# Two-layer transformer block on one core: the first layer's down product with tokens on partitions, gates applied in the scalar engine's copies

## The chip, the cores and the metric

The kernel runs on one core of a Trainium2 chip. The metric is device time in microseconds (us) of one execution. The median of three runs of the kernel before is 1977.41 us (1973.36 to 1984.65). The engines are named as the profile names them: PE is TensorE, DVE is VectorE, ACT is ScalarE, POOL is GpSimd, SP issues the DMAs.

## The reference

There are 16 sequences of 512 tokens with 128 features. Four residual steps follow one another, each on a layer norm of its input:

```
x = x + linear_attention(layernorm(x))         # layer 0: 16 heads of 8
x = x + experts0(layernorm(x))                 # layer 0: 8 routed experts, 2 of them per token, and 2 shared ones
x = x + softmax_attention(layernorm(x))        # layer 1: keys after the query are masked
x = x + experts1(layernorm(x))                 # layer 1: 16 experts, each takes its 512 best tokens
```

The change lies in the second step. With `xt` the normed tokens it is

```
scores  = softmax(xt @ gate_w.T)
_, idx  = top_k(scores + gate_bias, 2)
weights = take_along_axis(scores, idx)
for e in range(8):
    gate_e = sum(where(idx == e, weights, 0))                # one number per token
    h      = silu(xt @ w1[e].T) * (xt @ w3[e].T)
    y      = y + gate_e[:, None] * (h @ w2[e].T)
z = (silu(xt @ sw1.T) * (xt @ sw3.T)) @ sw2.T                # two shared experts of width 128, no gate
```

## The kernel before, in words

One sequence (512 tokens, four tiles of 128) is the unit of work. The kernel is written engine by engine with semaphores, and the order on each engine is the order of the code. Three stages of three sequences run side by side in two alternating phases. The helper `looped` writes the first and last phases out and puts the rest into a hardware loop of 13 turns, which holds one `x_phase` and one `y_phase`; at its end each engine jumps back, 12 times in all.

In `x_phase(f, b, t, g)` sequence `f` goes through the ten experts of layer 0, sequence `b` through the first pass of its attention scores (40 fills of three PSUM banks `ba`, each followed by row maxima on DVE, `maxima`), sequence `t` ends its attention (output product, rms norm, router logits) and sequence `g` starts (layer norm, transposes). In `y_phase(b, f, r, t)` sequence `b` makes its scores a second time with the maxima subtracted, ACT takes the exponentials and PE the outputs; `f` does its linear attention and, on DVE, the gates of its experts (`f_logits`, `f_gates`, `f_rank`); `r` makes queries and keys.

For each expert `e` of `f` there is a slot in `x_phase`. PE runs up to four fills, and between them `up` (w1, bank `fa[0]`), `up3` (w3, bank `fa[1]`), up to expert 7 `gate_rows` (spreads one gate row over 128 partitions, bank `fa[2]`), and `down` of the expert before. ACT takes `sil` out of `fa[0]` and copies the spread gates to `gb`. DVE multiplies `sil` by `fa[1]` (`product`, into `th`), then does steps of `t` and `g`, then the maxima of the slot's fills. POOL multiplies `th` by `gb` into `hh` (`gated`). `down` takes w2 as the stationary and all 512 tokens of `hh` as the moving operand and adds the ten experts up in one bank, `facc`, features on partitions. So at the end ACT copies the sum (`yT`), PE turns it back with four transposes, and DVE adds it to the residual `x1`.

The spread gates need gates with partitions as experts: `f_rank` splits each gate into three bf16 parts (`gparts`, L1242 to L1246), PE transposes them (`f_turn_gates`, L660), ACT copies them (`gT`), and `pick` is a constant that selects and sums the three parts of expert `e`.

The end of an `x_phase` has an order of its own. On PE slot 8 is `t_turn_row` and then `down` of expert 7; slot 9 is the last two fills, `t_router` (L740) and `down` of expert 8; then `turn_maxima` (L753), `down` of expert 9 and `f_turn_x`. `t_router` waits for ACT's copy of the turned rows, L1000. `turn_maxima` brings the maxima into the layout in which SP's DMAs write them into `QT`, for which the first score of the `y_phase` waits.

Of the kernel before, what the change touches and what calls it, by code (L numbers as in the profile page):

```python
# [19 lines left out]
P = 128  # L20
# [19 lines left out]
FILLS = HEADS // 2 * 5  # L40
ROW = D + E1
# [3 lines left out]
def build_kernel(nc, a, out):  # L45
    ctx = ExitStack()
    with ctx:
# [29 lines left out]
        pick = sb("pick", [P, E0, P], BF16)  # L77
# [58 lines left out]
        gres = sb1("gres", [P, Q, E0])  # L136
        gparts = sb1("gparts", [P, Q, PARTS, E0], BF16)
        gT = sb1("gT", [P, SEQ], BF16)
        sil = sb1("sil", [P, 2, SEQ])
        th = sb1("th", [P, 2, SEQ])  # L140
        gb = sb1("gb", [P, 2, SEQ])
        hh = sb1("hh", [P, 2, SEQ])
        yT = sb1("yT", [P, SEQ])
# [43 lines left out]
        def sb3(name, shape, dt=F32):  # L187
# [55 lines left out]
            s_kqn s_kvt s_kvm s_qT s_qnT s_kvo s_kvoc s_at0 s_x1 s_x1n s_T2 s_nT2 s_lgm s_lge s_exf s_lgx s_gp s_gTp s_gT  # L243
            s_h1 s_h3 s_gb s_gbc s_sil s_t s_h s_hs s_ym s_yT s_yTt s_x2 s_fc
# [177 lines left out]
        def _(pool):  # L422
# [15 lines left out]
            const(pool.memset(pick[:], 0.0))  # L438
            for part in range(PARTS):
                const(pool.affine_select(pick[:], pick[:], [[-1, E0], [0, P]], ALU.not_equal, 1.0, base=-E0 * part, channel_multiplier=1))  # L440
# [7 lines left out]
            const(pool.memset(mhalf[:], -0.5))  # L448
            pool.memset(gT[:], 0.0).then_inc(S["s_one"], 1)
# [5 lines left out]
            def gated(f, e):  # L455

                pool.wait_ge(S["s_t"], E0 * f + e + 1)
                pool.wait_ge(S["s_gbc"], E0 * f + e + 1)
                pool.wait_ge(S["s_ym"], U0 * f + max(e - 1, 0))
                pool.tensor_tensor(hh[:, e % 2], th[:, e % 2], gb[:, e % 2], ALU.mult).then_inc(S["s_h"], 1)  # L460

            def x_phase(f, b, t, g):
                for e in range(U0):
# [12 lines left out]
                    if f is not None and e < E0:  # L476
                        gated(f, e)
# [112 lines left out]

        def prob_block(h, blk):

            slot, k = (h // 2) % 3, h % 2
            if blk == 0:
                return probs[:, slot, 2 * k, :]
            if blk == 1:
                return probs[:, slot, 2 * k + 1, 0:384]
            if blk == 3:
                return probs[:, slot, 2 * k + 1, 384:512]
            return probs[:, slot, 4, 256 * k:256 * k + 256]  # L600

        @block.tensor
        def _(pe):
# [11 lines left out]
            def f_kvq(f, half):  # L615
                pe.wait_ge(S["s_nT1"], f + 1)
                for q in range(2 * half, 2 * half + 2):
                    if q == 0:
                        pe.wait_ge(S["s_hs"], SHARED * f)
# [36 lines left out]
            def f_turn_gates(f):  # L656
                pe.wait_ge(S["s_gp"], f + 1)
                apart(pe)
                for q in range(Q):
                    last = pe.transpose(fa[2][:].bitcast(BF16)[0:PARTS * E0, q * P:(q + 1) * P],  # L660
                                        gparts[:, q].rearrange("p c e -> p (c e)"), identb[:])
                last.then_inc(S["s_gTp"], 1)

# [8 lines left out]
            def gate_rows(b, e):  # L672

                if e == 0:
                    pe.wait_ge(S["s_gT"], b + 1)
                else:
                    pe.wait_ge(S["s_gbc"], E0 * b + e)
                pe.matmul(fa[2][:], lhsT=pick[:, e], rhs=gT[:], start=True, stop=True).then_inc(S["s_gb"], 1)

            def up3(b, e):  # L680

                if 0 < e <= E0:
                    pe.wait_ge(S["s_t"], E0 * b + e)
                elif e > E0:
                    pe.wait_ge(S["s_hs"], SHARED * b + e - E0)
                pe.matmul(fa[1][:], lhsT=w3[:, e], rhs=f_nT[:], start=True, stop=True).then_inc(S["s_h3"], 1)  # L686

            def down(b, e):
                if e < E0:
                    pe.wait_ge(S["s_h"], E0 * b + e + 1)  # L690
                else:
                    pe.wait_ge(S["s_hs"], SHARED * b + e - E0 + 1)
                if e == 0:
                    pe.wait_ge(S["s_yT"], b)
                    pe.wait_ge(S["s_vp"], b)
                pe.matmul(facc[:], lhsT=w2[:, e], rhs=hh[:, e % 2], start=e == 0, stop=e == U0 - 1).then_inc(S["s_ym"], 1)  # L696
# [60 lines left out]
            def x_phase(f, b, t, g):  # L757
# [21 lines left out]
                if f is not None:  # L779
                    f_turn_gates(f)  # L780
                for e in range(U0):
# [10 lines left out]
                    if f is not None and e == 0:  # L792
                        gate_rows(f, 0)
# [4 lines left out]
                    if f is not None and e + 1 < E0:  # L798
                        gate_rows(f, e + 1)
# [11 lines left out]
                if f is not None:  # L811
                    pe.wait_ge(S["s_yT"], f + 1)
                    for q in range(Q):
                        last = pe.transpose(facc[:, q * P:(q + 1) * P], yT[:, q * P:(q + 1) * P], ident[:])
                    last.then_inc(S["s_yTt"], 1)
# [154 lines left out]
        def _(act):  # L970
# [10 lines left out]
            def x_phase(f, b, t, g):  # L981
                for e in range(U0):
                    if f is not None:
                        act.wait_ge(S["s_h1"], U0 * f + e + 1)
                        if e < 2:
                            act.wait_ge(S["s_hs"], SHARED * f)
                        else:
                            act.wait_ge(S["s_t"], E0 * f + e - 1)
                        act.activation(sil[:, e % 2], fa[0][:], ACT.Silu).then_inc(S["s_sil"], 1)  # L989
                    if f is not None and e == 0:  # L990
                        copy(gT[0:PARTS * E0, :], fa[2][:].bitcast(BF16)[0:PARTS * E0, 0:SEQ], "s_gTp", f + 1, "s_gT")
                    if f is not None and e < E0:
                        act.wait_ge(S["s_h"], E0 * f + max(e - 1, 0))
# [641 lines left out]
```

## Time and profile before

| | us |
|---|---|
| median of the runs (lowest, highest) | 1977.41 (1973.36, 1984.65) |
| the profiled execution | 1980.44 |
| its span, first to last instruction | 1978.7 |
| PE busy (matmuls) | 1604.5 |
| DVE busy | 1237.3 |
| ACT busy | 778.6 |
| POOL busy | 501.7 |

The loop with its start and end fills the first four fifths of the span; the layer 1 experts are the rest, and the change does not touch them. "Busy" is an average over phases that are bound by different engines, so it has to be read phase by phase. In a timeline the bracket at the end of a row is the time for which the engine stood idle before it, and what released it; "issue" there means that the engine waited for no semaphore that the profile shows.

### The profile page before, as it was taken

The numbers are of one execution on the slowest core, as the hardware profiler recorded it, in microseconds if no ns is written. First come the engines' busy times: TensorE is split into PE (matmuls) and PEld (weight loads), VectorE is DVE, ScalarE is ACT, GpSimd is POOL, SyncE is SP. The second block draws the span as 40 slices with busy tenths as digits, with TensorE's granted clock in tenths as the row PEclk, the third lists the DMA queues.
The fourth block names the chain that finished last, engine by engine and source line by source line (L and its number), as shares of the span: only waits on it lengthen the run. The fifth ranks groups of instructions, "written<-read, shape, count | busy, mean of one in ns | idle before, by whom it ended". The sixth has DMA issues, their size and how long they took to land.

```text
span 1978.7 us, 33763 instructions
## 1 busy us (share of the span) xinstructions
PE 1604.5 (81%) x10090; PEld 903.9 (46%) x10136; DVE 1237.3 (63%) x3719; ACT 778.6 (39%) x1387; POOL 501.7 (25%) x487
## 2 busy tenths in 40 slices
PE   3889998898989898989898989898999751157675
PEld 2355454444444444444545444444454431145554
DVE  5566868585858585858585858676773638831111
ACT  1325252525253534444444444443445232323331
POOL 2321212121212121212121212122121020027886
PEclk7889999999999999999999999999999675578888
DMA  2022130303030303030302030202112100024444
GB/s 67 8 67 53 30 79 9 81 6 81 6 80 12 75 12 75 12 75 12 75 20 67 20 72 24 63 29 58 39 42 61 27 12 0 0 55 86 93 92 60
DMA packets 83242, 90.73 MB, mean 46 GB/s; under 512 B 19520, under 2 KB 73024, under 8 KB 78528
## 3 DMA queue, kind: packets, MB, share of 16 engines
q1 hardware_dynamic: 71872, 80.76, 16.3%
q0 software_dynamic: 11264, 8.92, 3.5%
q14 instruction: 84, 0.69, 0.1%
q8 instruction: 22, 0.36, 0.1%
HBM read 58.95 MB, written 29.92 MB: 45 GB/s over the span
## 4 chain that ended last, share of the span: by engine, by line
PE 50%; DVE 19%; issue 12%; POOL 5%; ACT 4%; DMA 2%; DVEq 1%; SPq 0%; ACTq 0%; POOLq 0%
PE ba L581 6%; PE bo L841 6%; PE ba L586 5%; PE facc L696 5%; PE fa L686 5%; PE fa L670 5%; POOL out L553 3%; ACT probs L1017 2%; DVE nm L1265 2%; PE ba L583 2%; DVE passed L1464 2%; PE ba L588 2%; POOL got L523 2%; PE ba L957 1%; PE bo L848 1%
## 5 line engine op out<-in xcount | busy, mean ns | idle before, releaser
L1017 ACT ACTIVATE probs<-ba 128x512 f32<-128x512 f32 x640 | 330.3, 636 | 97.3 <-PE ba L583 96.5
L586 PE MATMUL ba<-KT,QT 72*128 72x512 bf16 (+3 forms) x1024 | 256.3, 313 | 68.2 <-DVE nm L1265 43.5
L460 POOL TENSOR_TENSOR hh<-th,gb 128x512 f32<-128x512 f32 x128 | 162.0, 1266 | 582.4 <-ACT gb L973 317.2
L581 PE MATMUL ba<-QT,KT 75*128 75x512 bf16 (+3 forms) x1024 | 253.1, 309 | 35.4 <-ACT probs L1017 28.7
L1265 DVE TENSOR_REDUCE nm<-ba 128x1 f32<-128x512 f32 x256 | 174.8, 683 | 70.0 <-issue 38.3
L586 PEld LDWEIGHTS ba<-KT,QT 72*128 72x128 bf16 x1024 | 103.1, 101 | 224.9 <-DVE nm L1265 71.7
L588 PE MATMUL ba<-mask_q,identb 128*128 128x128 bf16 x1024 | 196.8, 226 | 0.0
L989 ACT ACTIVATE sil<-fa 128x512 f32<-128x512 f32 x160 | 95.4, 596 | 254.8 <-PE fa L670 254.7
L583 PE MATMUL ba<-mask_k,identb 128*128 128x128 bf16 x1024 | 195.2, 223 | 0.0
L670 PE MATMUL fa<-f_nT,w 128*128 128x512 f32 x320 | 183.8, 658 | 1.2 <-ACT sc L1048 1.2
L686 PE MATMUL fa<-f_nT,w 128*128 128x512 f32 x320 | 177.5, 637 | 0.1
L581 PEld LDWEIGHTS ba<-QT,KT 75*128 75x128 bf16 x1024 | 101.7, 99 | 155.7 <-ACT probs L1017 103.4
L696 PE MATMUL facc<-hh,w 128*128 128x512 f32 x320 | 166.2, 602 | 0.9
L841 PE MATMUL bo<-probs,vp 128*32 128x512 f32 (+3 forms) x2048 | 153.6, 441 | 0.8 <-DVE ao L1388 0.8
L1267 DVE TENSOR_REDUCE nm<-ba 128x1 f32<-128x384 f32 x256 | 140.8, 550 | 17.5 <-PE ba L588 17.0
L973 ACT ACTIVATE gb<-fa 128x512 f32<-128x512 f32 x128 | 76.5, 598 | 183.6 <-remote 92.3
L588 PEld LDWEIGHTS ba<-mask_q,identb 128*128 128x128 bf16 x1024 | 104.2, 102 | 81.1 <-issue 78.8
L453 POOL TENSOR_TENSOR b_rs<-b_ve,mhalf 128x4 f32<-128x4 f32 x48 | 48.5, 1010 | 330.5 <-DVE b_ve L1364 229.9
L1379 DVE COPY oT<-bo 128x512 f32<-128x512 f32 x64 | 44.2, 690 | 114.7 <-PE bo L841 113.6
L1572 DVE TENSOR_TENSOR ysum<-ba,fb 128x512 f32<-128x512 f32 x16 | 11.1, 692 | 158.5 <-PE ba L957 158.5
L553 POOL DMA_INDIRECT out<-contrib,cur x64 | 100.7, 1573 | 31.0 <-issue 18.6
L841 PEld LDWEIGHTS bo<-probs,vp 128*32 128x32 f32 x2048 | 60.5, 111 | 97.1 <-issue 68.5
(286 smaller groups left out, 2721.9 us busy)
## 6 DMA issues: line engine op xcount, KB each, us to landing
QT<-qk_parts SPq DMA_DIRECT2D x96, 192.0 KB
KT<-qk_parts SPq DMA_DIRECT2D x96, 192.0 KB
qk_parts<-qkp SPq DMA_DIRECT2D x32, 384.0 KB, 2.5
fc<-in_L_ffn_fc_weight SPq DMA_DIRECT2D x32, 256.0 KB, 3.1
xin<-in_L_attn_x SPq DMA_DIRECT2D x16, 256.0 KB, 7.1
qk_parts<-qkp SPq DMA_DIRECT2D x16, 256.0 KB, 2.7
out<-x SPq DMA_DIRECT2D x16, 256.0 KB, 2.3
xn_rows<-row SPq DMA_DIRECT2D x16, 256.0 KB, 2.4
```

Source lines behind the costliest of these rows:

```text
L460: pool.tensor_tensor(hh[:, e % 2], th[:, e % 2], gb[:, e % 2], ALU.mult).then_inc(S["s_h"], 1)
L553: pool.indirect_dma_start(out_rows, bass.IndirectOffsetOnAxis(cur[k][:, c:c + 1], 0), contrib[k % 2][:, c], None, compute_op=ALU.add).then ...
L581: pe.matmul(bank[:, col:col + w], lhsT=KT[0:K_ROWS, head, blk * P:(blk + 1) * P], rhs=QT[0:K_ROWS, head, blk * P:], start=True, stop=False)
L583: last = pe.matmul(bank[:, col:col + P], lhsT=identb[:], rhs=mask_k[:], start=False, stop=True)
L586: pe.matmul(bank[:, col:col + w], lhsT=QT[0:QK_ROWS, head, blk * P:(blk + 1) * P], rhs=KT[0:QK_ROWS, head, 0:w], start=True, stop=False)
L588: last = pe.matmul(bank[:, col + w - P:col + w], lhsT=identb[:], rhs=mask_q[:], start=False, stop=True)
L670: pe.matmul(fa[0][:], lhsT=w1[:, e], rhs=f_nT[:], start=True, stop=True).then_inc(S["s_h1"], 1)
L686: pe.matmul(fa[1][:], lhsT=w3[:, e], rhs=f_nT[:], start=True, stop=True).then_inc(S["s_h3"], 1)
L696: pe.matmul(facc[:], lhsT=w2[:, e], rhs=hh[:, e % 2], start=e == 0, stop=e == U0 - 1).then_inc(S["s_ym"], 1)
L841: last = pe.matmul(bo[32 * j:32 * j + 32, blk * P:], lhsT=vp[:, blk, 4 * k + j], rhs=prob_block(4 * k + j, blk), start=blk == 0, stop=blk ...
L1017: act.activation(probs[:, pair % 3, f_], ba[n % 3][:], ACT.Exp, scale=SCALE).then_inc(S["s_exp"], 1)
L1265: last = dve.tensor_reduce(nm[:, 3, h:h + 1], bank[:], X, ALU.max, negate=True)
```

## The change

The down product of an expert now has the tokens on partitions: each 128-token slice of `hh` is the stationary operand and w2 the moving one, four products of 128 columns in the place of one of 512. It goes to one of two banks in turn, `fa[2]` for even experts and `facc` for odd ones. The gate is then one number per partition, and ACT applies it as the scale of its copy out of the bank, four copies per routed expert (`gd`); expert 8 is copied in one piece without a scale; POOL adds each `gd` to the residual `x1`; expert 9 stays in `facc`, where DVE adds it to `x1`. DVE's `product` writes `hh` itself. `pick`, `gparts`, `gT`, `gb`, `th`, `yT` and what made them go.

```diff
 pool:
-                pool.wait_ge(S["s_t"], E0 * f + e + 1)
-                pool.wait_ge(S["s_gbc"], E0 * f + e + 1)
-                pool.wait_ge(S["s_ym"], U0 * f + max(e - 1, 0))
-                pool.tensor_tensor(hh[:, e % 2], th[:, e % 2], gb[:, e % 2], ALU.mult).then_inc(S["s_h"], 1)
+                pool.wait_ge(S["s_gd"], ADDED * f + e + 1)
+                pool.wait_ge(S["s_x1g"], ADDED * f + e)
+                pool.tensor_tensor(x1[:], x1[:], gd[:, e % 2], ALU.add).then_inc(S["s_x1g"], 1)
...
-                    if f is not None and e < E0:
-                        gated(f, e)
+                    if f is not None and e >= 2:
+                        add_gated(f, e - 2)
+                if f is not None:
+                    add_gated(f, E0)
 tensor:
-                pe.matmul(facc[:], lhsT=w2[:, e], rhs=hh[:, e % 2], start=e == 0, stop=e == U0 - 1)
+                for q in range(Q):
+                    last = pe.matmul(down_bank(e)[:, q * D:(q + 1) * D], lhsT=hh[:, e % 2, q * P:(q + 1) * P], rhs=w2[:, e],
+                                     start=True, stop=True)
...
-                    f_turn_gates(f)
-                        gate_rows(f, 0)
-                        gate_rows(f, e + 1)
-                    pe.wait_ge(S["s_yT"], f + 1)
-                    for q in range(Q):
-                        last = pe.transpose(facc[:, q * P:(q + 1) * P], yT[:, q * P:(q + 1) * P], ident[:])
 scalar:
-                        copy(gb[:, e % 2], fa[2][:], "s_gb", E0 * f + e + 1, "s_gbc")
+                    if f is not None and e >= 2:
+                        if e == 2:
+                            act.wait_ge(S["s_gates"], f + 1)
+                        act.wait_ge(S["s_ym"], U0 * f + e - 1)
+                        act.wait_ge(S["s_x1g"], ADDED * f + max(e - 3, 0))
+                        for q in range(Q):
+                            last = act.activation(gd[:, e % 2, q], down_bank(e - 2)[:, q * D:(q + 1) * D], ACT.Copy, scale=gates[:, q, e - 2:e - 1])
+                        last.then_inc(S["s_gd"], 1)
...
-                    copy(yT[:], facc[:], "s_ym", U0 * f + U0, "s_yT")
+                    act.wait_ge(S["s_x1g"], ADDED * f + ADDED - 2)
+                    copy(gd[:, E0 % 2], down_bank(E0)[:].rearrange("p (q d) -> p q d", q=Q), "s_ym", U0 * f + E0 + 1, "s_gd")
 vector:
-                fc.halves(lambda q: dve.scalar_tensor_tensor(gates[:, q], rank[:, q], TOPK - 0.5, sc[:, q], ALU.is_lt, ALU.mult))
-                fc.halves(lambda q: dve.tensor_copy(gparts[:, q, 0], gates[:, q]))
-                fc.halves(lambda q: dve.tensor_tensor(gres[:, q], gates[:, q], gparts[:, q, 0], ALU.subtract))
-                fc.halves(lambda q: dve.tensor_copy(gparts[:, q, 1], gres[:, q]))
                 fc.join()
-                dve.tensor_tensor(gparts[:, :, 2], gres[:], gparts[:, :, 1], ALU.subtract).then_inc(S["s_gp"], 1)
+                dve.scalar_tensor_tensor(gates[:], rank[:], TOPK - 0.5, sc[:], ALU.is_lt, ALU.mult).then_inc(S["s_gates"], 1)
...
-                    dve.wait_ge(S["s_yTt"], f + 1)
+                    dve.wait_ge(S["s_ym"], U0 * f + U0)
+                    dve.wait_ge(S["s_x1g"], ADDED * f + ADDED)
                     dve.tensor_tensor(x3_of(f), facc[:].rearrange("p (q d) -> p q d", q=Q), x1[:], ALU.add).then_inc(S["s_x2"], 1)
```

Three places show how the order moves. The first is DVE at the end of a `y_phase`, where `f_rank` ends and the engine branches into the loop (the jump back at the loop's end follows the same instructions). Before:

```order
L1239 TENSOR_REDUCE rank<-gt 128x16 x2
L1240 SCALAR_TENSOR_TENSOR gates<-rank,sc 128x16 x2
L1242 CAST gparts<-gates 128x2x8 x2
L1243 TENSOR_TENSOR gres<-gates,gparts 128x16 x2
L1244 CAST gparts<-gres 128x2x8 x2
L1246 TENSOR_TENSOR gparts<-gres,gparts 128x4x8
L1386 RECIPROCAL rden<-bo 128x16
L1388 TENSOR_TENSOR ao<-bo,rden 128x4x32
L278 UNCONDITIONAL_BRANCH
```

Now:

```order
L1210 TENSOR_TENSOR gt<-gt,eq 128x128 x2
L1211 TENSOR_REDUCE rank<-gt 128x16 x2
L1213 SCALAR_TENSOR_TENSOR gates<-rank,sc 128x32
L1350 RECIPROCAL rden<-bo 128x16
L1352 TENSOR_TENSOR ao<-bo,rden 128x4x32
L273 UNCONDITIONAL_BRANCH
```

Eight instructions fewer stand between the rank and the branch: the two halves of `gates` became one, and the seven of the bf16 parts are gone.

The second is ACT at the end of an `x_phase` (here the one after the loop; `sil` are the last three experts, `b_nT` the copy for which PE's `t_router` waits). Before:

```order
L989 ACTIVATE sil<-fa 128x512
L973 ACTIVATE gb<-fa 128x512
L989 ACTIVATE sil<-fa 128x512 x2
L1000 ACTIVATE b_nT<-bo,norm_col 128x512
L973 ACTIVATE nmT<-bo 24x512
L973 ACTIVATE yT<-facc 128x512
L973 ACTIVATE nmT<-bo 24x512
```

Now:

```order
L957 ACTIVATE sil<-fa 128x512
L964 ACTIVATE gd<-fa,gates 128x128 x4
L957 ACTIVATE sil<-fa 128x512
L964 ACTIVATE gd<-facc,gates 128x128 x4
L971 ACTIVATE b_nT<-bo,norm_col 128x512
L944 ACTIVATE nmT<-bo 24x512
L944 ACTIVATE gd<-fa 128x512
L944 ACTIVATE nmT<-bo 24x512
```

The four copies of expert 7, which wait for its `down`, came to stand between the last `sil` and `b_nT`.

The third is PE in slot 2 of an `x_phase` of the loop (`fa<-f_nT,w` is an `up3`, `bo<-w_o,b_nT` the output product of `t`, the `ba` rows a fill). Before:

```order
L686 MATMUL fa<-f_nT,w 128x512
L678 MATMUL fa<-gT,pick 128x512
L728 MATMUL bo<-w_o,b_nT 128x128 x4
L696 MATMUL facc<-hh,w 128x512
L767 REGISTER_ALU
L586 MATMUL ba<-KT,QT 128x256
```

Now:

```order
L666 MATMUL fa<-f_nT,w 128x512
L710 MATMUL bo<-w_o,b_nT 128x128 x4
L676 MATMUL facc<-w,hh 128x128 x4
L749 REGISTER_ALU
L578 MATMUL ba<-KT,QT 128x256
```

The gate rows are gone, and the down product stands at its place in four pieces.

## Rows read from the trace of the kernel before

**Rows 1.** Page, part 4: the chain that ended last, by engine.

```profile
PE 50%; DVE 19%; issue 12%; POOL 5%; ACT 4%; DMA 2%; DVEq 1%; SPq 0%; ACTq 0%; POOLq 0%
```

**Rows 2.** Windows of one x_phase: stretch, length, busy PE, PEld, DVE, ACT, POOL, PEclk, DMA.

```profile
683.90:703.90 20.00, 18.95 (x92) 10.29 (x95) 16.03 (x39) 5.64 (x10) 6.07 (x5) 0.91 0.05 13
703.90:723.80 19.90, 18.52 (x82) 8.37 (x82) 18.45 (x48) 4.18 (x7) 8.27 (x7) 1.00 0.00 1
723.80:734.10 10.30, 9.93 (x55) 5.61 (x53) 7.80 (x26) 3.54 (x6) 0.00 (x0) 1.00 0.01 2
```

**Rows 3.** DVE's timeline across the jump back: start, duration, engine, line, operation, [idle before].

```profile
678.93 0.36 DVE L1240 SCALAR_TENSOR_TENSOR gates<-rank,sc 128x16 f32<-128x16 f32 x2
679.30 0.35 DVE L1242 CAST gparts<-gates 128x16 bf16<-128x16 f32 x2
...
680.56 0.25 DVE L1386 RECIPROCAL rden<-bo 128x16 f32<-128x16 f32 x1
...
683.93 0.69 DVE L1265 TENSOR_REDUCE nm<-ba 128x1 f32<-128x512 f32 x1 [2.79 <-issue]
```

**Rows 4.** PE's timeline there: the first fill that needs a maximum.

```profile
684.68 0.49 PE L586 MATMUL ba<-KT,QT 72*128 72x384 bf16 x1 [3.02 <-DVE nm L1265]
```

**Rows 5.** All of L1265: idle before it by "issue", us and times.

```profile
  issue: 38.3, 12
```

**Rows 6.** DVE's timeline: the first maxima after three of the jumps back.

```profile
300.06 0.69 DVE L1265 TENSOR_REDUCE nm<-ba 128x1 f32<-128x512 f32 x1 [3.30 <-issue]
395.04 0.69 DVE L1265 TENSOR_REDUCE nm<-ba 128x1 f32<-128x512 f32 x1 [3.72 <-issue]
1359.77 0.69 DVE L1265 TENSOR_REDUCE nm<-ba 128x1 f32<-128x512 f32 x1 [3.02 <-issue]
```

**Rows 7.** Windows of 4 us behind the first two of these, columns as in rows 2.

```profile
300.50:304.50 4.00, 3.64 (x20) 2.02 (x22) 3.96 (x9) 1.36 (x3) 1.20 (x1) 1.00 0.01 2
395.50:399.50 4.00, 3.49 (x11) 1.86 (x13) 2.75 (x7) 0.61 (x2) 0.00 (x0) 0.50 0.00 2
```

**Rows 8.** PE's timeline in slots 2 and 3: L728, gate rows, down.

```profile
697.48 1.05 PE L728 MATMUL bo<-w_o,b_nT 128*128 128x128 f32 x8
...
702.29 0.38 PE L678 MATMUL fa<-gT,pick 128*128 128x512 bf16 x1
702.51 1.02 PE L696 MATMUL facc<-hh,w 128*128 128x512 f32 x2
```

**Rows 9.** PE's timeline at the end of the x_phase: down of expert 7, router, turn_maxima.

```profile
725.96 1.02 PE L696 MATMUL facc<-hh,w 128*128 128x512 f32 x2
...
727.50 1.01 PE L740 MATMUL bo<-router_w,b_nT 128*128 128x16 f32 x8
...
729.59 0.38 PE L753 MATMUL bo<-identb,nmp 128*24 128x128 bf16 x4
```

**Rows 10.** ACT's timeline: the copy for the router; a series of 32 with a per-partition operand.

```profile
726.16 0.69 ACT L1000 ACTIVATE b_nT<-bo,norm_col 128x512 f32<-128x512 f32 x1 [1.54 <-PE bo L734]
...
1720.76 19.74 ACT L1066 ACTIVATE stairs<-ramp,lows 128x512 f16<-128x512 f16 x32 [23.35 <-DVE ramp L1529]
```

**Rows 11.** ACT's groups by line and shape: busy and mean ns of a copy.

```profile
L973 ACT ACTIVATE gb<-fa 128x512 f32<-128x512 f32 x128 | 76.5, 598 | 183.6 <-remote 92.3 <-PE fa L678 58.9 <-POOL hh L460 32.4
...
L973 ACT ACTIVATE kvo<-fa 128x128 f32<-128x128 f32 x16 | 5.2, 325 | 0.0
```

**Rows 12.** DVE's and POOL's timelines in slot 5: two like instructions, one beside POOL.

```profile
710.05 0.15 DVE L1293 TENSOR_TENSOR b_ve<-b_mv,b_rs 128x4 f32<-128x4 f32 x1
710.31 1.26 DVE L1294 TENSOR_TENSOR b_ve<-b_ve,b_rs 128x4 f32<-128x4 f32 x1
...
710.29 1.26 POOL L460 TENSOR_TENSOR hh<-th,gb 128x512 f32<-128x512 f32 x1 [0.92 <-DVE th L1254]
```

**Rows 13.** DVE's and POOL's timelines at the start of the program.

```profile
4.83 6.88 DVE L1149 MEMSET KT<- 32x8192 bf16 x1 [1.76 <-issue]
...
4.80 3.56 POOL L440 TENSOR_SCALAR_AFFINE_SELECT pick<-pick 128x1024 bf16<-128x1024 bf16 x3
```

More of the change, by code:

```diff
@@ L40 @@
 FILLS = HEADS // 2 * 5
+ADDED = U0 - 1
 ROW = D + E1
@@ L437, in _ @@
             const(pool.affine_select(mask_k[:], mask_k[:], [[1, P]], ALU.is_ge, MASKED, base=0, channel_multiplier=-1))
-            const(pool.memset(pick[:], 0.0))
-            for part in range(PARTS):
-                const(pool.affine_select(pick[:], pick[:], [[-1, E0], [0, P]], ALU.not_equal, 1.0, base=-E0 * part, channel_multiplier=1))
             const(pool.memset(blockdiag[:], 1.0))
@@ L589, in scores, with down_bank @@
             last.then_inc(S["s_st" if by_key else "s_S"], 1)
+        def down_bank(e):
+            return facc if e % 2 else fa[2]
         def prob_block(h, blk):
@@ L618, in f_kvq @@
                     if q == 0:
-                        pe.wait_ge(S["s_hs"], SHARED * f)
+                        pe.wait_ge(S["s_hh"], U0 * f)
+                    if q == 1:
+                        pe.wait_ge(S["s_gd"], ADDED * f)
                     if q == 3:
@@ L670, in up @@
                 pe.matmul(fa[0][:], lhsT=w1[:, e], rhs=f_nT[:], start=True, stop=True).then_inc(S["s_h1"], 1)
[L672 to L678, printed above, removed]
             def up3(b, e):
[L682 to L685, printed above, removed]
+                if e > 0:
+                    pe.wait_ge(S["s_hh"], U0 * b + e)
                 pe.matmul(fa[1][:], lhsT=w3[:, e], rhs=f_nT[:], start=True, stop=True).then_inc(S["s_h3"], 1)
             def down(b, e):
[L689 to L694, printed above, removed]
-                    pe.wait_ge(S["s_vp"], b)
-                pe.matmul(facc[:], lhsT=w2[:, e], rhs=hh[:, e % 2], start=e == 0, stop=e == U0 - 1).then_inc(S["s_ym"], 1)
+                pe.wait_ge(S["s_hh"], U0 * b + e + 1)
+                if e == 1:
+                    pe.wait_ge(S["s_x2"], b)
+                    pe.wait_ge(S["s_vp"], b)
+                elif e >= 2:
+                    pe.wait_ge(S["s_gd"], ADDED * b + e - 1)
+                for q in range(Q):
+                    last = pe.matmul(down_bank(e)[:, q * D:(q + 1) * D], lhsT=hh[:, e % 2, q * P:(q + 1) * P], rhs=w2[:, e],
+                                     start=True, stop=True)
+                last.then_inc(S["s_ym"], 1)
             def r_turn(r):
@@ L791, in x_phase @@
                         up(f, e + 1)
-                    if f is not None and e == 0:
-                        gate_rows(f, 0)
                     next_fill()
@@ L810, in x_phase @@
                     f_turn_x(g)
-                if f is not None:
-                    pe.wait_ge(S["s_yT"], f + 1)
-                    for q in range(Q):
-                        last = pe.transpose(facc[:, q * P:(q + 1) * P], yT[:, q * P:(q + 1) * P], ident[:])
-                    last.then_inc(S["s_yTt"], 1)
             def y_phase(b, f, r, t):
@@ L984, in x_phase @@
                         act.wait_ge(S["s_h1"], U0 * f + e + 1)
[L985 to L988, printed above, removed]
+                        act.wait_ge(S["s_hh"], U0 * f + max(e - 1, 0))
                         act.activation(sil[:, e % 2], fa[0][:], ACT.Silu).then_inc(S["s_sil"], 1)
[L990 to L993, printed above, removed]
-                        copy(gb[:, e % 2], fa[2][:], "s_gb", E0 * f + e + 1, "s_gbc")
+                    if f is not None and e >= 2:
[6 more added lines that the diff above has]
+                        last.then_inc(S["s_gd"], 1)
                     if t is not None:
```

35 lines of the change are left out of this document (8 added, 27 removed).

## The prediction

> **What bounds the kernel now.** I read the page's chain first: half of what ends last is PE's work, a fifth DVE's, an eighth is "issue", time in which an engine waits for nothing that is shown [rows 1]. An average over phases says little here, so the second view is a table of windows over one `x_phase`, where the change lies. In its first 20 us PE works 18.95 us and DVE 16.03: DVE waits for PE. In the next 20 DVE has 18.45 of 19.9, and PE, which may be three banks ahead, 18.52: DVE sets the pace there. At the end, ten us in which the maxima go out and the experts are closed, PE has 9.93 of 10.3 [rows 2]. A gain on ACT or POOL is worth nothing by itself; one on PE counts in the first half and at the end, one on DVE in the second half.
>
> The third view is DVE's timeline across the loop's jump back. DVE has ended the gates of `f` and the last norm, then it stands for 2.79 us without a semaphore to wait for, and only then takes its first maxima [rows 3]. This happened 12 times for 38.3 us, 3.2 us each [rows 5], as often as the loop jumps. PE has made three fills by then, needs a bank back and stands for 3.02 us [rows 4]. What DVE does before the jump is thus on the path of all engines.
>
> Behind that stand PE often runs at the lower of its clock's two levels: in the 4 us after the second jump the granted clock is 0.50 (1.2 GHz), after the first it stays at 1.00 (2.4 GHz) [rows 7]. What this costs I take from the starts of the turns. The first turn, undisturbed, is 94.98 us with a stand of 3.72 at its end, so 91.26 without; the mean of the eleven turns between the first and the last start is 1059.71 / 11 = 96.34, less a mean stand of (38.3 - 3.3) / 11 = 3.2, so 93.15 [rows 5, 6]. The clock costs 1.9 us a turn on average.
>
> **The change part by part.**
>
> *Gates on DVE.* Nine instructions after the rank become one. Before, the pair L1240 starts at 678.93 and the last norm, L1386, at 680.56 [rows 3]. The one instruction left can start where the second of the pair did, half of 0.36 later at 679.11, and takes about 0.2; L1386 then starts at 679.3, its bank having been ready. That is 1.3 us (1.1 to 1.5), and the stand at the jump moves forward with it, so PE's wait of 3.0 becomes about 1.7 to 2.0 (the transposes of the gates on PE, which go too, stood inside that wait and cost nothing). `f_rank` runs 16 times: 16 x 1.3 = 21 us less. I count the four runs outside the jumps too, since DVE is what is waited for there.
>
> Why the stand should move and not stay: the Trainium skill's page "Runtime: NRT & Kernel Launch", section "Instruction fetch mechanics", says that a taken branch out of the small instruction window has to fetch its target before anything goes on. The trace fits that: 12 stands for 12 jumps. By that rule the stand keeps its length and begins earlier. That it does not is a rival below.
>
> *Gate rows on PE.* Eight products of 0.22 us (702.29 to 702.51) go [rows 8]. Five stand in the half in which DVE waits for PE, and I count one of the later three, where DVE still waits once: 6 x 0.22 = 1.3. Against them stand the down products: a product of eight instructions with 128 columns took 1.05 us where the present down takes 1.02 [rows 8]; 0.03 for each of five is 0.15. Net 1.15 in each of the 15 phases that hold both fills and experts: 17 us less. Bounds: 0.3 if each down also exposes a tenth of a microsecond of weight loads, 1.7 if all eight rows count.
>
> *The chain of an expert.* POOL's product leaves the way from `product` to `down`, and a wait of `product` for the down two experts before comes in. Neither shows: PE takes `down` a slot later, and DVE reaches `product` only after the maxima of a fill that PE issues behind that very `down`. If this cover failed, each slot would wait up to a down, 1.0 us.
>
> *ACT at the end of the phase.* This is the part that costs. The four scaled copies of expert 7 stand before L1000, the copy for which the router waits, and they wait for the down of expert 7. That down starts at 725.96 and is done 1.02 later, at 726.98 [rows 9]; L1000 ran at 726.16 before, ahead of all that [rows 10]. No row shows a 128-column copy with a scale per partition. A plain one takes 0.325 and a plain one of 512 columns 0.598 [rows 11]; with a scale per partition 512 columns take 0.69 [rows 10], 0.09 more; and in the series of 32 (19.74 us at 0.7 each) one starts 0.61 after the other, 0.09 before the end of the first [rows 10]. So I take 0.325 + 0.09 - 0.09 a copy, 1.3 for four (0.9 if the scale is free, 1.7 if nothing overlaps). A release takes 0.06: maxima ended at 684.62, the fill began at 684.68 [rows 3, 4]. L1000 starts at 726.98 + 0.06 + 1.3 = 728.35, ends at 729.04, and the router starts at 729.1 in the place of 727.50 [rows 9]. PE stands 1.6 us. The router and the down of expert 8 follow one another then; I count 1.01 and 1.02 [rows 9], each less 0.15, since behind a product of 0.38 the next begins after 0.22 [rows 8]: 1.73. So `turn_maxima` starts at 730.83, not at 729.59 [rows 9]: 1.25 us late. All that follows, the transposed maxima, their DMAs, the first scores of the `y_phase`, hangs on it. It holds for the 14 phases with both `t` and `f`: 14 x 1.25 = 17.5 us more (0.5 to 1.7 each; nothing speaks for a gain, the copy is later in any case).
>
> *The sum's close.* ACT's `yT` copy, four transposes and DVE's sum become ACT's copy of expert 8, POOL's add of 1.26 (as L460 [rows 12]) and DVE's sum. The four transposes of PE stood in the time in which the DMAs of the maxima are under way, so their going brings nothing; the new chain is about as long as the old. I put it at 0 (0.5 either way).
>
> *POOL's adds against DVE.* L1294 takes 1.26 us where L1293, the same operation on the same size, takes 0.15: it ran while POOL worked on L460 [rows 12]. So POOL's 1.26-us instructions can hold up DVE for their whole length. Before there are eight per phase, begun right after `product`, just when DVE turns to such steps; now there are nine, begun when the copies end. In slot 5 the new add has to queue behind POOL's other work and ends about half a microsecond earlier than L460 did; in slots 6 and 7 it comes nearer to small casts and to the row's centring. I take 0, with 1.1 either way.
>
> *The clock.* With PE standing 2 instead of 3.4 us some of the falls should not come, or be shorter; the new stand at the router may bring one. I take a third of the 1.9: 12 x 0.6 = 7 us less (0 to 23).
>
> *The start.* POOL no longer makes `pick`; that ran beside DVE's fill of KT, 6.88 us against 3.56, which ends later [rows 13]. Nothing; without that cover 4 to 5 us once.
>
> Sum: -21 - 17 + 17.5 - 7 = -27.5. The profiled execution took 1980.4 and its span 1978.7; it lies 3 above the median of the runs. So 1953 against the profiled one, 1950 against the median.
>
> **The rivals.**
>
> *The clock stays up.* All 1.9 us come back in 12 turns: 23 in the place of 7, 1934. For it: the first turn shows that the fall is not a must [rows 7]. Against it: PE still stands some 2 us.
>
> *The stand does not move.* If the wait at the jump ends at a time set by something else, 12 of the 16 gate terms go (+16) and the clock term with them (+7): 1973. For it: its length varies, 2.79 to 3.72 [rows 3, 6]. Against it: one stand per jump, and none elsewhere.
>
> *Slower: POOL blocks DVE more often.* Place: the second half, in slots 5 to 9, where DVE sets the pace and has its small steps between SBUF tensors (squares, casts of the maxima, centrings). Price: up to 1.1 us for each hit [rows 12]. With two more hits per phase (2 x 14 x 1.1 = 31 against 27.5) the gain is gone; with three more, 46, it ends at 1950 + 46 = 1996, about 1995. The Trainium skill's page "SBUF — State Buffer", section "Who interferes with whom", speaks for it: a DVE instruction with two SBUF inputs, or a cast or scalar operation in a two-port mode, is shut out for a whole POOL instruction, whoever comes first having the ports. By that rule casts, which met no POOL work so far, can be hit too. Rows 12 agree for two inputs. Against it: before, POOL started at the worst moment in each slot, and the new adds start at a moment that shifts.
>
> **How the numbers follow.** The forecast has 0.55 and a range of its own of 1936 to 1965. The clock rival has 0.20, the stand that does not move 0.13, the slower one 0.08; 0.04 is for what I have not seen. The range 1926 to 1981 takes in the first three. A measurement of this kernel tells 0.5% (10 us) from no change: below 1967.5 lie nearly all of the forecast, the clock rival and little of the third, 0.74; above 1987 the slower rival and a bit, 0.09; the rest, 0.17, is between.
>
> **What would show it.** Right: L1265's stand by "issue" still near 3 us and 12 times, PE's wait before the fill behind it near 2; an `x_phase` first half with less DVE idle; ACT's L1000 starting after the copies of expert 7, and a new wait of PE of 1 to 2 us before the router. Wrong: a stand that grew by what DVE saved; `turn_maxima` no later against the last fill; DVE's small steps at 1 us and more in slots 6 to 9; a router wait that brings the clock down to 1.2 GHz at the start of the `y_phase`.

## The result, and the profile after

The changed kernel took 2008.73 us (median of four runs, 2002.83 to 2012.69), the kernel before 1980.47 in the same session: a ratio of 1.0144 (95% interval 1.0102 to 1.0186). The forecast was 1950, a gain of 27 us, with 1926 to 1981 as its range; the change made the kernel slower. The profiled execution has a span of 2005.5 us.

Where the 27 us of the spans come from is seen turn by turn. The table is read off the timelines of PE and DVE, as the mean of the twelve turns that begin with a jump back: from PE's first fill of an `x_phase` to the first maxima, to the last fill, to `turn_maxima`, to the first score of the `y_phase`, and to the last turned outputs.

| us per turn | first maxima | last fill | turn_maxima | first score | end of y | turn |
|---|---|---|---|---|---|---|
| before | 5.88 | 43.55 | 2.25 | 4.54 | 39.91 | 96.32 |
| after | 6.53 | 43.22 | 3.52 | 5.06 | 40.72 | 99.23 |

A turn is 2.91 us longer, 35 for twelve. What stands ahead of the first jump back is 5.3 us shorter (the first turn behind a jump starts at 288.8 and not at 294.1), what stands behind the twelve turns about 3.

The first column is the surprise. Here is DVE's timeline across a jump of the changed kernel, which answers to [rows 3].

```profile
784.16 0.29 DVE L1210 TENSOR_TENSOR gt<-gt,eq 128x128 f32<-128x128 f32 x1 [0.23 <-DVE gt L1210]
...
784.94 0.19 DVE L1213 SCALAR_TENSOR_TENSOR gates<-rank,sc 128x32 f32<-128x32 f32 x1
785.05 0.25 DVE L1350 RECIPROCAL rden<-bo 128x16 f32<-128x16 f32 x1
785.33 0.29 DVE L1352 TENSOR_TENSOR ao<-bo,rden 128x128 f32<-128x128 f32 x1
790.83 0.69 DVE L1228 TENSOR_REDUCE nm<-ba 128x1 f32<-128x512 f32 x1 [5.21 <-issue]
```

The last norm starts 0.11 us behind the gates (0.2 in the forecast), and then DVE stands for 5.21 us in the place of 2.79. This idle time at the jump is called the stand from here on. PE's wait for the first maximum, 3.02 before [rows 4], is 4.73 (means of the twelve: 3.42 and 4.39), and the clock behind it is at 1.2 GHz; all stands together, 38.3 before [rows 5], are 58.3 (PE's timeline, then the idle time of all L1228, then a window of 4 us, columns as in [rows 2]).

```profile
791.58 0.50 PE L578 MATMUL ba<-KT,QT 72*128 72x384 bf16 x1 [4.73 <-DVE nm L1228]
```

```profile
  issue: 58.3, 12
```

```profile
791.50:795.50 4.00, 3.92 (x13) 2.13 (x14) 3.15 (x8) 0.60 (x1) 0.00 (x0) 0.50 0.01 4
```

What DVE waits for is in the DMA view, which counts packets by queue: queue 14 brings code (queue 8 does too, but nothing in these twelve turns). First before, the microsecond behind DVE's branch at 680.93 and the rest of the stand; then after, the 2.2 us behind the branch at 785.42 and the rest.

```profile
q1 hardware_dynamic: 289, 0.14, 82.5%
...
q14 instruction: 1, 0.01, 1.0%
```

```profile
q1 hardware_dynamic: 402, 0.27, 68.7%
...
q14 instruction: 2, 0.02, 2.9%
```

In the first stretch of each pair a burst of data transfers is running (queue 1: the second half of `QT` and `KT`, then the next `x`), and no code comes. It comes when the burst thins out: 1.00 us behind the branch before, 2.22 after (means of the twelve jumps: 1.31 and 1.87). The burst does not follow DVE. It ends 3.9 us behind PE's first fill before, and after the change 3.8 in nine of the turns, though DVE branches 1.46 us behind that fill and no longer 2.49. In the other three turns, which follow a `y_phase` made 1.6 us longer by a fall of the clock, it ends at 2.4, and the stand is 3.6 to 3.9 us and not 4.9 to 5.8. And after the change there are two packets, not one: 0.41 apart, the second of 1.03 us. The page counts 12 more in the whole run, as many as there are jumps (before, then after):

```profile
q14 instruction: 84, 0.69, 0.1%
```

```profile
q14 instruction: 96, 0.79, 0.2%
```

A packet is 8.2 KB by these rows. In the turn at 586 the later packets start when DVE has begun 14, 145 and 276 of the 412 instructions of its loop (waits and register steps included). DVE itself is held up, by 0.2 to 0.3 us, ahead of instructions 268 and 396 in each of the twelve turns, 128 apart (the second is the idle time in the row at 784.16 above). So a new piece of code begins there, and the last one some 15 instructions ahead of the jump. A packet starts soon behind each such place (276 behind 268); the one that 396 brings is for code that the jump leaves out, and the jump's target queues behind it. In the kernel before, the later packets start at 103, 231 and 350 of 441, and nothing is held up near the end. From the start of the first packet to the next DVE instruction it is 2.1 us with one packet and 3.2 with two.

At the end of the phase PE's rows (answering to [rows 9]) are as forecast: the router waits for its copy, L971, which now stands behind the four scaled ones, and `turn_maxima` is 3.52 us behind the last fill. But then the clock falls to 1.2 GHz, in 8 of the 12 turns, as the product of 2.08 shows and the window of 3.4 us behind it.

```profile
638.51 1.06 PE L722 MATMUL bo<-router_w,b_nT 128*128 128x16 f32 x8 [1.21 <-ACT b_nT L971]
...
640.82 2.08 PE L676 MATMUL facc<-w,hh 128*128 128x128 f32 x8
```

```profile
640.80:644.20 3.40, 3.40 (x18) 2.86 (x16) 0.80 (x2) 1.48 (x3) 1.27 (x1) 0.51 0.02 5
```

Over the twelve turns the mean granted clock (0.98 and 0.95 in these windows) fell, and PE was busy for the same time:

```profile
294.10:1449.90 1155.80, 1045.97 (x6805) 558.71 (x6841) 822.51 (x2509) 501.24 (x913) 238.75 (x216) 0.98 0.18 44
```

```profile
288.80:1479.50 1190.70, 1046.08 (x7369) 632.77 (x7369) 809.94 (x2412) 546.37 (x1189) 254.05 (x228) 0.95 0.18 43
```

The clock has two levels, 1.0 and 0.5; in the trace's clock records 55 us of these turns are at the lower one before and 116 after.

### The profile page after: what moved, and what is told of

Read it like the earlier page. It is cut to its first block, busy times and chain, and to the rows that moved or that the text cites. A ratio compares the mean times of both kernels' runs of the same rounds, so it can differ in the third digit from the quotient of the medians.

```text
span 2005.5 us, 35172 instructions
## 1 busy us (share of the span) xinstructions
PE 1589.7 (79%) x10840; PEld 991.6 (49%) x10840; DVE 1222.1 (61%) x3591; ACT 838.7 (42%) x1755; POOL 517.6 (26%) x498
## 4 chain that ended last, share of the span: by engine, by line
PE 51%; DVE 17%; issue 16%; POOL 6%; ACT 5%; DMA 3%; DVEq 1%; SPq 1%; ACTq 0%; POOLq 0%
PE fa L666 6%; PE bo L812 6%; PE ba L573 6%; PE ba L578 5%; PE fa L660 5%; PE facc L676 3%; PE fa L676 3%; POOL out L545 3%; PE ba L580 2%; ACT probs L989 2%; DVE passed L1428 2%; PE ba L575 2%; DVE nm L1228 2%; PE ba L928 1%; POOL got L515 1%
## 5 line engine op out<-in xcount | busy, mean ns | idle before, releaser
L450 POOL TENSOR_TENSOR x<-x,gd 128x512 f32<-128x512 f32 x144 | 182.4, 1267 | 756.8 <-ACT gd L964 715.6
L578 PE MATMUL ba<-KT,QT 72*128 72x512 bf16 (+3 forms) x1024 | 261.0, 318 | 71.5 <-DVE nm L1228 54.5
L1228 DVE TENSOR_REDUCE nm<-ba 128x1 f32<-128x512 f32 x256 | 174.3, 681 | 85.3 <-issue 58.3
L666 PE MATMUL fa<-f_nT,w 128*128 128x512 f32 x320 | 186.1, 665 | 12.3 <-DVE hh L1220 11.9
L660 PE MATMUL fa<-f_nT,w 128*128 128x512 f32 x320 | 182.0, 652 | 1.2 <-ACT sc L1020 1.2
L964 ACT ACTIVATE gd<-facc,gates 128x128 f32<-128x128 f32 x256 | 73.0, 367 | 155.1 <-PE facc L676 155.1
L1220 DVE TENSOR_TENSOR hh<-sil,fa 128x512 f32<-128x512 f32 x160 | 108.4, 678 | 16.0 <-PE fa L676 8.8
L964 ACT ACTIVATE gd<-fa,gates 128x128 f32<-128x128 f32 x256 | 73.0, 368 | 92.7 <-PE fa L676 92.7
```

Source lines behind the costliest of these rows:

```text
L450: pool.tensor_tensor(x1[:], x1[:], gd[:, e % 2], ALU.add).then_inc(S["s_x1g"], 1)
L578: pe.matmul(bank[:, col:col + w], lhsT=QT[0:QK_ROWS, head, blk * P:(blk + 1) * P], rhs=KT[0:QK_ROWS, head, 0:w], start=True, stop=False)
L660: pe.matmul(fa[0][:], lhsT=w1[:, e], rhs=f_nT[:], start=True, stop=True).then_inc(S["s_h1"], 1)
L964: last = act.activation(gd[:, e % 2, q], down_bank(e - 2)[:, q * D:(q + 1) * D], ACT.Copy, scale=gates[:, q, e - 2:e - 1])
L1228: last = dve.tensor_reduce(nm[:, 3, h:h + 1], bank[:], X, ALU.max, negate=True)
```

## The experiments

The theory: the stand at the jump is a fetch of code. It waits behind the burst of data DMAs, so its end is tied to the burst and not to DVE; and where the code of the loop happens to lie decides how many packets it takes. The rivals stand with each run. Each kernel was timed beside the kernel before on one chip; the ratio is to that. Turns and their parts are taken as in the table above.

**e1, e7: the place of the code.** 46 instructions ahead of the changed kernel's loop put its first instruction at the same place in a piece of code as before; 52 ahead of the loop before put a piece's start near its end (104 waits there; two waits become one instruction).

```diff
+            for _ in range(92):
+                dve.wait_ge(S["s_pad"], 1)
             dve.memset(vp[:, :, :, HD:HD + 1], 1.0).then_inc(S["s_pad"], 1)
```

> The changed kernel; VectorE's program has 46 more instructions at its very start (waits on a semaphore that stands long before), nothing in the loop is altered. Only the place of its loop in its program moves. Theory (fetch of code): in the changed kernel VectorE's loop ends 7 instructions behind the start of a new 8-KB piece of code, whose useless fetch goes ahead of the one for the jump's target; so two pieces are fetched at a jump and the first maxima come about 1.05 us later. With 46 more the piece starts far from the loop's end: the instruction packets of queue 14 go from 96 to about 84, the stand before the first maxima from a mean of 4.86 to 3.8 us, 12 x 1.05 = 12.6 us less, and up to 10 more if the longer falls of TensorE's clock behind it get shorter: 1986 to 1996. Rival (the stand ends when the DMAs of the phase end, whatever the code): 96 may change, the stand and the time stay, 2009 within 4.

> The kernel before with 52 more instructions at the start of VectorE's program, so that a new 8-KB piece of code begins as far ahead of the loop's end as in the changed kernel. Theory: instruction packets of queue 14 go from 84 to 96, two at each jump; from the first packet's start to the first maxima 3.1 us and not 2.0. If the burst of DMAs ends where it did, the stand goes from 3.2 to about 4.2 us and the time up by 12 to 30 us, to 1990 to 2008. Rival (as in e1 the burst's end moves with it): stand within 0.3 us of 3.2, time within 5 of 1979.

e1: 1982.48, ratio 1.0014 (1.0002 to 1.0027), against 1.0144 without the move: 26 us won with instructions that do nothing. The packets came out as expected, 84 (the piece of the changed kernel begins 15 instructions ahead of the jump and not 7, which doesn't bear on the move); the stand did not:

```profile
  issue: 56.8, 12
```

It is 4.73 us and not 3.8. From the first packet to the maxima it is 2.1 us again, but that packet starts 2.8 us behind the branch on average and not 1.9. DVE reaches the branch 0.3 us earlier, since it is no longer held up just ahead of it, the burst ends 0.5 later against PE's first fill (why isn't shown), and DVE waits for the difference. Of the 2.71 us that a turn is shorter 0.45 are in the first maxima and 1.76 in the fills. Of these 1.0 is a cast that before the move met POOL. DVE's rows of the changed kernel and of e1 at the same place of the loop's first phase, which no jump precedes, and POOL's:

```profile
226.49 1.19 DVE L1280 CAST nmp<-nm 128x32 bf16<-128x32 f32 x1
...
226.38 1.26 POOL L450 TENSOR_TENSOR x<-x,gd 128x512 f32<-128x512 f32 x1 [2.92 <-ACT gd L964]
```

```profile
229.62 0.17 DVE L1282 CAST nmp<-nm 128x32 bf16<-128x32 f32 x1
...
229.87 1.27 POOL L450 TENSOR_TENSOR x<-x,gd 128x512 f32<-128x512 f32 x1 [3.27 <-ACT gd L964]
```

With POOL 0.11 us ahead the cast takes 1.19, with POOL 0.25 behind it takes 0.17. The nine kinds of small DVE steps between SBUF tensors (casts, centrings, `b_sc`, `b_ve`) took 6.61 us a turn before, 6.91 after, 5.57 in e1.

e7: 1997.73, ratio 1.0098 (1.0077 to 1.0118), within the expected time, but only half by the expected way. There are 97 packets, and in nine turns 3.2 us from the first to the maxima (in three the useless packet comes ahead of the branch). But the stand is 3.56, between the two theories: DVE, now held up for 0.36 us 15 instructions ahead of the jump, branches 0.35 later, nearer to the burst's end. Of the 1.47 us that a turn is longer 0.72 are in the first maxima and 0.83 in the `y_phase`, where DVE is held up for 0.3 in every turn and the clock falls more often:

```profile
  issue: 42.7, 12
```

**e2: the burst.** SP issues the last part of the burst later.

```diff
             with sp.Fori(1, BATCH - 2) as i:
+                sp.wait_ge(S["s_red"], FILLS * i + 1)
+                apart(sp)
                 load_x(i + 2)
```

> The changed kernel; SP issues the load of the next sequence (256 KB, the last piece of the burst of DMAs that stands at the jump back) only when the first maxima of the phase are taken. Theory (the fetch of the jump's target waits behind the burst): the burst ends about 1.3 us earlier against TensorE's first fill, the first instruction packet starts 0.6 to 1.0 us behind VectorE's branch and not 1.9, the stand before the first maxima goes from 4.86 to about 3.7 us; 12 to 15 us less, and up to 10 more by the clock: 1984 to 1997. Rival (the fetch has a latency of its own of about 2 us): stand and time as in the changed kernel, 2009 within 4. A second rival: x comes too late for the layer norm in slot 2, VectorE waits there and the time rises.

1989.21, ratio 1.0046 (1.0033 to 1.006): as expected, 3.73 us a stand. The code's place is that of the changed kernel; only the burst is shorter. Of the 2.02 us that a turn is shorter 1.13 are in the first maxima, 1.15 in the fills, where less of the time is at 1.2 GHz. In the three turns in which the burst is over at the branch, the next instruction follows 2.8 to 2.9 us behind it; in the others 3.8 to 4.9. In these three the useless packet has also come ahead of the branch, so about 1.1 us of that difference is the packet and not the burst.

```profile
  issue: 44.8, 12
```

**e3: the router's copy** ahead of the copies of expert 7, not behind.

```diff
+                    if t is not None and e == 9:
+                        act.wait_ge(S["s_T4"], t + 1)
+                        act.activation(b_nT[:], bo[:], ACT.Copy, scale=norm_col[:]).then_inc(S["s_nT4"], 1)
                     if f is not None and e >= 2:
```

> The changed kernel; in the last slot ScalarE copies the turned rows for the router ahead of the four scaled copies of expert 7, as in the kernel before. Theory: the router waits no more, turn_maxima starts 2.25 us behind the last fill and not 3.52; 14 x 1.27 = 18 us less, and the falls of the clock right behind turn_maxima (9 in 12 turns) go, some 0.5 us each: about 1986 (1980 to 1994). Rival (the wait only changes place: the copies of expert 7 come later, POOL's last adds and the sum for the next norm with them): the y_phase starts earlier but its keys and queries later, 2000 to 2009.

1982.68, ratio 1.001 (1.000 to 1.002). `turn_maxima` is 2.22 us behind the last fill, the first score 4.54 behind that in every turn, the `y_phase` 40.25: a turn is 2.36 us shorter, 1.30 of them the wait, and about 1.0 the falls of the clock behind it. The stand stays (60.4 in all).

**e4, e5, e6: the jump elsewhere.** DVE's own loop is cut ahead of its second outputs in the `y_phase`. `False` ends a `y_phase` behind `f_kvm`, and `y_tail` is the rest. In e5 it is done to the kernel before; e6 is e4 with e3.

```diff
-            looped(dve, x_phase, y_phase)
...
+            x_phase(2, 1, 0, 3)
+            y_phase(1, 3, 2, 0, False)
+            with dve.Fori(1, BATCH - 3) as i:
+                fc.b = i + 2
+                y_tail(i, i + 2, i + 1, i - 1)
+                x_phase(i + 2, i + 1, i, i + 3)
+                y_phase(i + 1, i + 3, i + 2, i, False)
```

> The changed kernel; VectorE's own loop is cut at another place: its jump back stands in the middle of the y_phase, ahead of the second outputs, where it waits 4.65 us for TensorE anyway; one more turn of its code stands ahead of the loop, and it jumps 11 times. The order of its instructions is the same. Theory (the stand is the fetch of the jump's target): no stand ahead of the first maxima, which come 1.4 to 2.5 us behind the first fill as in the turn that is entered without a jump, and not 6.53; 12 x 4.5 = 54 us less, and the falls of the clock behind it (9 of 6.83 us) go too, up to 30 more: 1925 to 1955. Rival (the stand is at the start of the phase for another reason): nothing changes there, 2009. Second rival: the stand is longer than the 4.65 us that cover it: a part of the gain goes, 1960 to 1985.

> The kernel before, with the same cut as in e4: VectorE jumps back in the middle of the y_phase. Beside e4 it shows what the change is worth where no stand and little of the clock's falls mix in. Theory (in the changed kernel the gates on VectorE and the gate rows on TensorE are gains, which the stand at the jump gave back): here the first maxima come about 2.5 us behind the first fill, as in the turn entered without a jump, 1.2 later than in e4 (1.26), the fills take 41 to 41.7 against 40.5, the router's wait of 1.27 is not there: 1915 to 1940, e4's 1913.8 being up to 1.3% less. Rival (the change is a loss of its own, by the router's wait and POOL's adds): 1890 to 1910, less than e4.

> e4 and e3 together: the jump in the middle of the y_phase and the router's copy first. Theory (they act at different places): e4's turn_maxima start 3.72 us behind the last fill and the first score 4.91 behind that; with e3's 2.22 and 4.54 a turn is 1.9 us shorter, 12 x 1.9 + 2 x 1.3 = 25 less than 1913.8: 1885 to 1895. Rival (with the stand gone the end of the y_phase waits for something else, the sum of the first layer's experts among it): 1900 to 1914.

e4: 1913.83, ratio 0.9673 (0.9658 to 0.9688), more than expected. DVE's timeline at the start of an `x_phase`, and at the new place of the jump:

```profile
652.72 0.29 DVE L1391 TENSOR_TENSOR ao<-bo,rden 128x128 f32<-128x128 f32 x1
652.93 0.68 DVE L1228 TENSOR_REDUCE nm<-ba 128x1 f32<-128x512 f32 x1
...
634.14 0.69 DVE L1382 COPY oT<-bo 128x512 f32<-128x512 f32 x1 [4.64 <-PE bo L812]
```

The maxima follow at once, and at the jump DVE waits 4.64 us for PE, as long as at this place in the changed kernel, where no jump stood. The fetch lies inside: its packet starts 1.7 us behind the branch. The first maxima come 1.26 us behind the first fill, the fills take 40.48 and a turn 90.89. Of the 8.34 us that a turn is shorter 5.27 are in the first maxima and 2.74 in the fills, in which the clock no longer falls.

e5: 1921.1, ratio 0.9716 (0.9695 to 0.9738), within the expected time. The kernel before gains 57 us by this cut. So the change itself, with the router's wait in it, is worth 0.4% (7 us) where no stand mixes in, by the two ratios. e6: 1885.41, ratio 0.9528 (0.9508 to 0.9549), within the expected time; its turn is 88.82. With the router's copy in order the change is worth 36 us, 1.9% of e5. This version beats both kernels.

**e8: POOL's sums.**

```diff
-                pool.tensor_tensor(x1[:], x1[:], gd[:, e % 2], ALU.add).then_inc(S["s_x1g"], 1)
+                pool.tensor_tensor(x1[:, :, 0:1], x1[:, :, 0:1], gd[:, e % 2, :, 0:1], ALU.add).then_inc(S["s_x1g"], 1)
```

> The changed kernel; POOL's sums take one column of each of the four tiles and not 128, so nearly all of the gated products are left out of the result; semaphores and order are the same. Theory (what e1 won is not the stand, which was 4.73 us against 4.86, but that VectorE's cast of the maxima no longer comes just behind the start of a POOL sum and is held up for 1 us): the cast of the maxima, b_sc and b_ve take 0.17 us each and not 1.18, 0.95 and 0.59, 2.2 us less of VectorE per phase in its own half; the stand stays at 4.9; 12 x 1.5 to 14 x 2.2 less, 1975 to 1992. Rival (e1's gain is the place of the code alone): VectorE's steps get shorter, the time stays above 2000.

1962.98, ratio 0.9925 (0.990 to 0.995): more than expected. The stand stays (5.04 us), the small steps take 4.67 us a turn in the place of 6.91, and the fills 40.54 in the place of 43.22. The rest is the clock, whose mean in the loop is 0.97. The router's wait is still there (`turn_maxima` 3.58 us behind the last fill), but the clock falls behind it in one turn of twelve and not in eight.

**e9, e10: a longer end on DVE,** in the changed kernel and in e4.

```diff
                 dve.scalar_tensor_tensor(gates[:], rank[:], TOPK - 0.5, sc[:], ALU.is_lt, ALU.mult).then_inc(S["s_gates"], 1)
+                dve.tensor_tensor(sq[:], sq[:], sq[:], ALU.subtract)
```

> The changed kernel; behind the gates VectorE has one more instruction, which nobody waits for: a subtraction of a 128x1024 tile from itself, an estimated 1.1 us (twice the 0.55 of a 128x512 one is the most). It takes back most of the 1.3 us by which the change made this place shorter. Theory (the stand ends when the burst of DMAs and the fetch behind it are done, whatever VectorE had before it): the stand gets shorter by what the instruction takes, 4.86 to about 3.8 us, the first maxima stay 6.5 us behind the first fill and the time stays: 2009 within 6. Rival (the step of the prediction: what VectorE does ahead of the jump is on the path of all engines): the stand stays, 16 x 1.1 = 18 more: 2027.

> e4 (jump in the middle of the y_phase) with the same instruction as in e9. Theory: without a stand the end of VectorE's y_phase is what the first maxima wait for, so here it counts: first maxima 2.3 us behind the first fill and not 1.26, 12 x 1.05 to 14 x 1.1 = 13 to 16 more than 1913.8: 1926 to 1930, less if part of it lies beside TensorE's own three fills. Rival (a step there is free in any case): 1914.

The instruction takes 1.22 us. e9: 2012.37, ratio 1.0163 (1.0146 to 1.018). The loop is as long as without it (a turn of 99.20 against 99.23); what stands ahead of the first jump is 5.2 us longer. The stand gave back only part:

```profile
  issue: 52.4, 12
```

That is 4.37 us, 0.49 less; the first maxima are 0.32 later and the fills take 0.56 less, so the turn as a whole shows nothing of the 1.22, but not by the stand alone; why the fills are shorter isn't shown. The time is within the expected 6 us for the theory, by a way that is only in part the theory's. e10: 1936.27, ratio 0.978 (0.9763 to 0.9796), 22 more than e4 and more than expected: 1.14 a turn in the first maxima, and 0.37 in the fills, where the cast meets POOL again (1.36 us for the two casts of a phase, 0.34 in e4).

## Why the prediction was wrong

*Gates on DVE: the step that failed.* "The stand at the jump moves forward with it" was priced at 21 us of gain. In the loop it was 0.65 us a turn of loss, 8 in all; only in the phases entered without a jump did the first maxima come 1.0 to 1.5 earlier. DVE's branch did come 1.02 us earlier (1.34 in e1, where nothing is held up ahead of it), near the 1.3 of the forecast, but the stand behind it grew by 1.66. Two things stood behind that. The stand's end is tied to the burst of DMAs (shown by e2, in part by e9), so the first packet started 0.56 us later behind the branch. And fewer instructions in and ahead of the loop moved its code, so that one more packet stood ahead of the target: 1.1 us, shown in the packets of the changed kernel, e1 and e7. The rival "the stand does not move" had the mechanism half right, with "a time set by something else", and 0.13; it allowed no longer stand. The Trainium skill's page "Runtime: NRT & Kernel Launch", section "Instruction fetch mechanics", was read as giving a stand of fixed length; it states no length. It also says that a sequencer fetches the next block while it runs the present one; the useless packet ahead of the jump fits that, and the prediction didn't weigh it. That page of the Trainium skill gives blocks of 16 KiB, 256 instructions; for DVE this trace has packets of 8.2 KB on queue 14, 128 instructions apart, and the measurement decides (queue 8 has packets of 16.4 KB, as the page says).

*The clock.* Forecast 7 us of gain; it became a large part of the loss: 116 us of the turns at 1.2 GHz and not 55. In the changed kernel the fills behind a stand of under 4 us have 3.4 us at the lower level, those behind one of 4.9 or more 5.9 to 6.8. With the router's wait came falls behind `turn_maxima`, which the prediction named only among the signs of failure. Without the wait (e3) there are none, worth 0.52 a turn up to the first score; but e8 has the wait and nearly none, so the wait isn't enough by itself, and what else it takes is open. In some turns the clock falls at the end of the `y_phase`, which then takes 41.8 us and not 40.2, behind waits that other turns have too; why there is open.

*Gate rows on PE.* Forecast 1.15 a phase; the loop's first phase, which no jump precedes and which has no fall, shows 0.43 (41.74 to 41.31). The slots in which PE is waited for gained 0.17 each, near the 0.22 of the row; five of them and not six count, the first product starts 0.3 later against the maxima, and the second half gives back 0.2. In e4 beside e5 it is 1.0, of which 0.7 lies in DVE's small steps.

*ACT at the end of the phase.* Forecast 1.25 later, measured 1.27. The estimate from the two shapes held: the copies take 0.367 each, 1.14 for four.

*POOL's adds.* Forecast 0 with 1.1 either way. The sum of the small steps rose by 0.3, as the stalls of two steps went and those of three others came. But e1 and e8 show that 1.3 to 2.2 us of DVE's time a turn hang on where and how long the adds run, and DVE sets the pace there; the products of the kernel before cost it 1.9 by the same steps (6.61 against e8's 4.67). The Trainium skill's page "SBUF — State Buffer", section "Who interferes with whom", says that a cast can be shut out for a whole POOL instruction; the row of 1.19 beside POOL's start 0.11 earlier agrees, which no row before showed.

*The sum's close and the start* cost nothing that shows.

So the loop loses 35 us and the rest of the program wins 8 of them back, which leaves the 27 by which the spans differ. The 35 are terms that act on one another: 8 in the first maxima, 15 in the router's wait, 16 behind it up to the end of the `y_phase` (about 4 of them the 0.3 us at instruction 268, which e1 hasn't), less 4 won in the fills. e3 takes back 26 and e1 26 by themselves; e4 takes back 95, more than the change lost, since the stand was there before.

## What to carry to other kernels

An engine's idle time by "issue" at a loop's jump is not part of its path as work is: read which DMA queue the code comes on, what traffic stands ahead of it and when that ends, before pricing work saved ahead of it. Put the jump of an engine's loop where that engine waits anyway; here, for DVE, this was worth 2.8% of the kernel before (e5), more than the change it was found with. A time that moves by 1% when instructions without effect are added is a sign that the place of the code and the meetings of engines decide, and a change of that size has to be judged with these taken away.

## What the runs showed of the hardware

Fetches of code wait for data transfers. In all 36 jumps of the kernel before, the changed one and e1 the first packet for the jump starts within 0.4 us of the end of the burst, 0.6 to 3.7 us behind the branch; where no burst is left (three turns of e2) it starts 1.0 us behind it. A packet asked for earlier does come through inside the burst (e1, 1.5 us ahead of the branch, 0.6 long), so it queues and isn't shut out. A new piece of code that begins some 15 instructions ahead of a jump costs about 1.1 us at a jump where its packet comes behind the branch (all twelve of the changed kernel, nine of e7). Where DVE runs without a break into a new piece, every 128 instructions, it is held up for 0.2 to 0.4 us (the changed kernel at 268 and 396, e7 at 298 and 426, in every turn). ACT, whose loop in the changed kernel has 189 instructions, jumps back without a stand: 0.26 us from its branch to the next instruction.
